# An attention block on one core: how the turned probabilities go through DRAM, and where values, transposes and the weighted sum stand

## The chip, the core and the metric

The kernel runs on one core of a Trainium2 chip. The metric is the device time of one execution in microseconds (us), as the median of several runs. A profile of one further execution shows when each engine worked: TensorE (PE, with its weight loads as PEld), VectorE (DVE), ScalarE (ACT), GpSimd (POOL) and SyncE (SP, which here issues DMAs only; its DMA queue is written SPq).

## What is computed

A transformer block on x of 32 sequences x 256 tokens x 256 features, with a context of 32 x 256 x 192: self attention, cross attention and a gated feed-forward part, 16 heads of 64, all in float32.

```python
h = _ln(x, g1, be1)
x = _attn(h, h, Wq1, Wk1, Wv1, Wo1, bo1) + x
h = _ln(x, g2, be2)
x = _attn(h, context, Wq2, Wk2, Wv2, Wo2, bo2) + x
h = _ln(x, g3, be3)
y = h @ Wp + bp
a, gate = (y[..., :FF_HID], y[..., FF_HID:])
x = a * jax.nn.gelu(gate, approximate=False) @ W2 + b2 + x
```

`_attn` projects q, k and v, takes the softmax of q k^T / 8 per head, weights v with it, and projects with Wo.

## The kernel before

Three parts run one after the other: `attention` for self attention (names begin with `self_`), `attention` again for cross attention (`cross_`), and `feed_forward` (`ff_`). The change touches `attention` alone. Most products are made of three matmuls on a high and a low part of each operand (`h_hi`, `h_lo` and so on), so each operand is copied once (the high part, on ScalarE) and subtracted once (the low part, on VectorE or GpSimd).

Each attention part goes over 32 sequences, and each sequence over 8 pairs of heads. One pair is one step, and all engines run the same list of steps (`sequences`): the first sequence (FIRST), a hardware loop over the middle ones (LOOP), the last (LAST), and a drain. In step p an engine works on several pairs at once, each at its own lag behind the projected pair: scores one step later, exponentials two, turn three (`TURNED`), load four (`LOADED`), weighted sum five (`WEIGHTED`), output projection six (`PROJECTED`). The order of the work on an engine is the order in which `step` writes it; engines meet by semaphores only.

The path of one pair, numbered s over the whole part:

- TensorE projects q and k into the one PSUM bank `ps_qk` (L640), 12 matmuls in self attention and 11 in cross. ScalarE copies it to `qk_hi` (L472), VectorE makes `qk_lo` (`low_parts`, L558). The next projection waits for `qk_lo`.
- TensorE makes the scores (L726), VectorE the negated maxima of each half (L549), ScalarE the exponentials and their sums (L412), VectorE the inverse of the sums (L574), GpSimd scales the probabilities, one half at a time (L379).
- VectorE transposes 32 x 32 blocks of both halves at once into `blocks`, which has two slots (`turn`, L568). The blocks have to change partitions, which goes through the DRAM tensor `turns`: SyncE stores the tile by four DMAs of 32 partitions each, in rows of 1 KB (`store_turn`, L301), and loads it back by one DMA of 128 partitions with rows of 4 KB into `probs_t`, a ring of four (`load_turn`, L309).
- TensorE makes the weighted sum (L744), ScalarE and VectorE its high and low part (L463, L585), TensorE the output projection (L704), which adds up over the 8 pairs in `ps_y`.

On SyncE a step is `load_turn` of pair s-1 and then `store_turn` of pair s. The load waits for the semaphore of the pair's stores, and everything on SyncE stands in one row, so the stores of pair s are not issued before the load of s-1 is.

V is projected in parts of a quarter of its columns and one of two tiles of tokens: `V_PARTS` lists for steps 0 to 6 what is made, one part each, both tiles in step 4, nothing in step 7. All use the bank `ps_misc`, from which ScalarE copies (`copy_v`, L451). The transposes of the next sequence's normalized input (step 6, L662) and context (step 5) use the same bank, after the V part of their step, so they wait for its copy.

For the next sequence, VectorE does `norm_stats` in step 2 and `norm_apply` in step 3, ScalarE `high_h` and `high_context` in step 7, GpSimd `low_h` and `low_context` in step 7, ahead of the two scalings, and the residual with its bias (`residual`, L360) right behind them.

Of the kernel before, what the change touches and what calls it, by code (L numbers as in the profile page):

```python
# [24 lines left out]
F32 = mybir.dt.float32  # L25
# [23 lines left out]
SCORES, EXPS, TURNED, LOADED, WEIGHTED, PROJECTED = 1, 2, 3, 4, 5, 6  # L49
# [7 lines left out]
V_PARTS = ((0, (0,)), (0, (1,)), (1, (0,)), (1, (1,)), (2, (0, 1)), (3, (0,)), (3, (1,)))  # L57
V_READY = (2, 4, 5, 7)
# [82 lines left out]
def attention(nc, tag, x_in, ctx_in, x_out, weights, bo, gamma, beta, prefetch, yout, y_stored, before):  # L141
# [7 lines left out]
    with ExitStack() as es:  # L149
# [50 lines left out]
        turns = nc.dram_tensor(tag + "turns", [RING, QUADS, QUAD, QUADS, TURN], F32).ap()  # L200
# [58 lines left out]
        def stored_count(b, q):  # L259

            return 16 * QUADS * (PAIRS // 2 * b + q // 2 + 1)
# [4 lines left out]
        def _(sp):  # L266
# [28 lines left out]
            def store_turn(b, p):  # L295

                s = PAIRS * b + p - TURNED
                slot = (p - TURNED) % RING
                sp.wait_ge(turned, s + 1)
                for i in range(QUADS):  # L300
                    sp.dma_start(turns[slot, :, :, i].rearrange("j k n -> k j n"),  # L301
                                 blocks[QUAD * i:QUAD * (i + 1), slot % 2].rearrange("k (j n) -> k j n", j=QUADS)
                                 ).then_inc(turn_stored[slot % 2], 16)

            def load_turn(b, p):
# [3 lines left out]
                sp.dma_start(probs_t[:, slot], turns[slot].rearrange("j k i n -> (j k) (i n)")  # L309
                             ).then_inc(turn_loaded[slot], 16)  # L310
# [22 lines left out]
        def _(pool):  # L333
# [28 lines left out]
            def step(b, p, part):  # L362
# [3 lines left out]
                if part in (FIRST, LOOP) and p == 7:  # L366
                    low_h(b + 1)
                    if cross:
                        low_context(b + 1)
                if part != DRAIN and p == PROJECTED + 1:  # L370
                    residual(b)
                if alive(part, p, EXPS):
# [3 lines left out]
                    for h in range(2):  # L376
                        pool.wait_ge(inv_ready, 2 * s + h + 1)
# [16 lines left out]
        def _(act):  # L394
# [50 lines left out]
            def copy_v(b, p):  # L445

                quarter, tiles = V_PARTS[p]
                act.wait_ge(v_done, len(V_PARTS) * b + p + 1)
# [6 lines left out]
            def step(b, p, part):  # L455
# [24 lines left out]
                if part != DRAIN and p < len(V_PARTS):  # L480
                    copy_v(b, p)
                if part in (FIRST, LOOP) and p == 6:
# [14 lines left out]
        def _(dve):  # L497
# [25 lines left out]
            def extras(b, p, part):  # L523
# [7 lines left out]
                if part in (FIRST, LOOP):  # L531
# [4 lines left out]
                    if p == 5 and cross:  # L536
# [40 lines left out]
            def step(b, p, part):  # L577
# [568 lines left out]
```

## Time and profile before

| what | us |
|---|---|
| median of 3 runs | 3448.78 |
| lowest and highest of them | 3444.27, 3453.83 |
| the profiled execution | 3446.99 |
| its span, first to last instruction | 3445.2 |
| self attention, first pair's store to last (issues) | 31.1 to 1392.1 |
| cross attention, first pair's store to last (issues) | 1433.9 to 2849.0 |

The span is what the rows further on divide up. "Busy" is the time in which an engine had an instruction running, matmuls overlapping one another. A wait names what ended it. An issue of a DMA on SPq takes SyncE some tenths of a microsecond; its landing is when its semaphore has its full count.

### The profile page before, as it was taken

The page shows a single profiled execution, that of the slowest core. Times are in us where ns is not written, and L with a number is a line of the kernel's source. Part 1 is how long each engine was busy: PE and PEld are TensorE (multiplying, and loading weights), DVE is VectorE, ACT ScalarE, POOL GpSimd, SP SyncE. Part 2 cuts the span into 40 slices and gives each one's busy share as a digit, 9 for nine tenths or more (in the row PEclk, how much of TensorE's full clock was granted, in tenths as well). Part 3 has the DMA queues.
Part 4 walks back from the last instruction along what each step waited for, and adds up shares of the span by engine and source line. Part 5 has one row for each costly group of instructions (what it writes and reads, how often), then busy time and mean ns, then how long its engine had stood idle before and what let it go on. Part 6 is the DMA issues. An engine that isn't in the chain of part 4 may idle for free. (4 is left out here: it accounts for less than half of the span.)

```text
span 3445.2 us, 81835 instructions
## 1 busy us (share of the span) xinstructions
PE 3157.5 (92%) x25600; PEld 2633.6 (76%) x25600; DVE 2473.8 (72%) x4811; ACT 1891.2 (55%) x6063; POOL 1362.1 (40%) x1295
## 2 busy tenths in 40 slices
PE   7999999999999999689889988899989887999999
PEld 6877888777888777577777777777777766888888
DVE  7777777777777777577777777777777775556555
ACT  6666666665666665456556566566656552233222
POOL 4444444444444444344444444444444441001010
PEclk9999999999999999799999999999999998999999
DMA  7676677767677766577677676777767762000010
GB/s 234 213 220 213 215 216 217 215 211 217 213 218 216 213 216 214 163 215 209 211 209 217 208 218 211 215 210 216 219 207 213 214 207 60 31 30 30 24 37 19
DMA packets 464425, 625.02 MB, mean 181 GB/s; under 512 B 57728, under 2 KB 397056, under 8 KB 464128
## 3 DMA queue, kind: packets, MB, share of 16 engines
q1 hardware_dynamic: 460256, 624.09, 59.4%
q10 hardware_dynamic: 4128, 0.41, 0.1%
q8 instruction: 23, 0.38, 0.0%
q14 instruction: 18, 0.15, 0.0%
HBM read 330.71 MB, written 293.60 MB: 181 GB/s over the span
## 5 line engine op out<-in xcount | busy, mean ns | idle before, releaser
L379 POOL TENSOR_TENSOR cross_probs<-cross_probs,cross_row_inv 128x512 f32<-128x512 f32 x512 | 531.7, 1048 | 586.1 <-DVE cross_row_inv L574 570.7
L379 POOL TENSOR_TENSOR self_probs<-self_probs,self_row_inv 128x512 f32<-128x512 f32 x512 | 531.9, 1049 | 542.2 <-DVE self_row_inv L574 542.0
L412 ACT ACTIVATE cross_probs<-cross_ps_s,cross_neg_max 128x256 f32<-128x256 f32 x1024 | 474.6, 473 | 69.2 <-DVE cross_neg_max L549 66.2
L412 ACT ACTIVATE self_probs<-self_ps_s,self_neg_max 128x256 f32<-128x256 f32 x1024 | 474.1, 472 | 43.8 <-DVE self_neg_max L549 41.0
L549 DVE TENSOR_REDUCE self_neg_max<-self_ps_s 128x2 f32<-128x512 f32 x512 | 327.7, 681 | 116.8 <-PE self_ps_s L726 116.3
L549 DVE TENSOR_REDUCE cross_neg_max<-cross_ps_s 128x2 f32<-128x512 f32 x512 | 327.8, 681 | 110.3 <-PE cross_ps_s L726 110.2
L568 DVE STREAM_TRANSPOSE self_blocks<-self_probs 128x1024 f32<-128x1024 f32 x256 | 316.5, 1236 | 111.3 <-POOL self_probs L379 108.7
L568 DVE STREAM_TRANSPOSE cross_blocks<-cross_probs 128x1024 f32<-128x1024 f32 x256 | 316.5, 1237 | 103.1 <-POOL cross_probs L379 100.5
L744 PE MATMUL cross_ps_o<-cross_probs_t,cross_v 128*64 128x256 f32 x2048 | 283.6, 398 | 72.2 <-DMA cross_probs_t<-cross_turns 71.8
L463 ACT ACTIVATE cross_o_hi<-cross_ps_o 128x256 fp32r<-128x256 f32 x256 | 98.5, 385 | 447.8 <-PE cross_ps_o L744 447.8
L463 ACT ACTIVATE self_o_hi<-self_ps_o 128x256 fp32r<-128x256 f32 x256 | 98.5, 385 | 391.7 <-PE self_ps_o L744 391.7
L744 PE MATMUL self_ps_o<-self_probs_t,self_v 128*64 128x256 f32 x2048 | 281.0, 395 | 18.2 <-DMA self_probs_t<-self_turns 17.8
L950 ACT ACTIVATE ff_u_hi<-ff_gated 128x512 fp32r<-128x512 f32 x128 | 81.0, 632 | 300.9 <-PE ff_ps_y L1090 214.2
L744 PEld LDWEIGHTS cross_ps_o<-cross_probs_t,cross_v 128*64 128x64 f32 x2048 | 132.2, 138 | 146.4 <-issue 64.2
L640 PE MATMUL cross_ps_qk<-cross_h_hi,cross_hi_wq 128*128 128x256 f32 x512 | 172.0, 336 | 44.1 <-DVE cross_qk_lo L558 39.0
L910 POOL TENSOR_TENSOR ff_xres<-ff_xt,ff_b 128x1024 f32<-128x1024 f32 x16 | 38.5, 2406 | 437.5 <-DMA out<-ff_yout 437.5
L412 ACT ACTIVATION_READ_ACCUMULATOR cross_probs<-cross_ps_s,cross_neg_max 128x1 f32 x1024 | 210.4, 206 | 0.0
L640 PE MATMUL self_ps_qk<-self_h_hi,self_hi_wq 128*128 128x256 f32 x512 | 172.5, 337 | 41.1 <-DVE self_qk_lo L558 33.0
L412 ACT ACTIVATION_READ_ACCUMULATOR self_probs<-self_ps_s,self_neg_max 128x1 f32 x1024 | 209.8, 205 | 0.0
L640 PEld LDWEIGHTS cross_ps_qk<-cross_h_hi,cross_hi_wq 128*128 128x128 f32 x512 | 97.3, 190 | 146.6 <-issue 97.9
L1034 DVE TENSOR_TENSOR ff_u_lo<-ff_gated,ff_u_hi 128x512 fp32r<-128x512 f32 x128 | 115.8, 904 | 129.4 <-ACT ff_u_hi L950 129.4
L640 PEld LDWEIGHTS self_ps_qk<-self_h_hi,self_hi_wq 128*128 128x128 f32 x512 | 97.4, 190 | 142.7 <-issue 99.7
(166 smaller groups left out, 10332.6 us busy)
## 6 DMA issues: line engine op xcount, KB each, us to landing
self_turns<-self_blocks SPq DMA_DIRECT2D x1024, 128.0 KB, 3.5
self_probs_t<-self_turns SPq DMA_DIRECT2D x256, 512.0 KB, 3.8
cross_turns<-cross_blocks SPq DMA_DIRECT2D x1024, 128.0 KB, 3.5
cross_probs_t<-cross_turns SPq DMA_DIRECT2D x256, 512.0 KB, 3.8
self_xt<-in_x SPq DMA_DIRECT2D x32, 256.0 KB, 3.4
self_xres<-in_x SPq DMA_DIRECT2D x32, 256.0 KB, 3.8
after_self_attention<-yout SPq DMA_DIRECT2D x32, 256.0 KB, 3.6
cross_xt<-after_self_attention SPq DMA_DIRECT2D x32, 256.0 KB, 3.9
```

The source lines that it names most:

```text
L379: pool.tensor_tensor(probs[:, slot % 2, h], probs[:, slot % 2, h], scale, ALU.mult).then_inc(probs_ready, 1)
L412: last = act.activation(probs[:, slot % 2, h, t], scores[:, slot % 2, h, t], ACT.Exp, bias=neg_max[:, slot % 2, i:i + 1], accum_out=row_su ...
L463: act.activation(o_hi[:, slot], ps_o[:, 0:SEQ], ACT.Copy).then_inc(o_hi_ready, 1)
L549: nc.vector.tensor_reduce(neg_max[:, slot, r], scores[:, slot, h], AX_X, ALU.max, negate=True).then_inc(neg_max_ready, 1)
L568: nc.vector.transpose(blocks[:, slot % 2].rearrange("p (j a q) -> p a j q", j=QUADS, q=QUAD), probs[:, slot % 2].rearrange("p h t (k j q) ...
L640: last = nc.tensor.matmul(out, m[:, p * P:(p + 1) * P], a, start=i == 0, stop=i == len(passes) - 1)
L744: last = nc.tensor.matmul(ps_o[DHEAD * h:DHEAD * (h + 1), 0:SEQ], v[:, k, c:c + DHEAD], turned_t[:, h, k], start=k == 0, stop=k == TT - 1)
L910: pool.tensor_tensor(xres[:], xt[:, parity], bias, ALU.add).then_inc(xres_ready, 1)
L950: act.activation(u_hi[:, slot], gated[:, slot], ACT.Copy).then_inc(u_hi_ready, 1)
L1034: nc.vector.tensor_tensor(u_lo[:, slot], gated[:, slot], u_hi[:, slot].bitcast(F32), ALU.subtract).then_inc(u_ready, 1)
```

## The change

- `turns` gets the layout of the tile itself. The store is one DMA of 128 partitions in rows of 4 KB. The load is four DMAs of 32 partitions each, in rows of 1 KB, and does the change of partitions.
- `WEIGHTED` is 6 and `PROJECTED` 7, so the weighted sum and all behind it come one pair later, and the drain has seven steps. The result (`yout`) and what goes with it on SyncE move along.
- V is made in six parts at steps 0, 1, 2, 4, 6 and 7: steps 2 and 4 make both tiles, steps 3 and 5 none. The transposes of the context are in step 3 and those of h in step 5; the V part behind each waits until `ps_misc` has been read.
- Within the projections of h, the terms with `h_lo` are last, and TensorE waits for `h_lo` only ahead of them, in the first step of a sequence.
- On VectorE `turn` stands behind `low_parts`.
- On GpSimd `low_h` and `low_context` stand between the two scalings of step 7, and `residual` stands in step 2 of the next sequence.

```diff
-SCORES, EXPS, TURNED, LOADED, WEIGHTED, PROJECTED = 1, 2, 3, 4, 5, 6
+SCORES, EXPS, TURNED, LOADED, WEIGHTED, PROJECTED = 1, 2, 3, 4, 6, 7
...
-V_PARTS = ((0, (0,)), (0, (1,)), (1, (0,)), (1, (1,)), (2, (0, 1)), (3, (0,)), (3, (1,)))
-V_READY = (2, 4, 5, 7)
+V_PARTS = ((0, (0,)), (0, (1,)), (1, (0, 1)), (2, (0, 1)), (3, (0,)), (3, (1,)))
+V_STEPS = (0, 1, 2, 4, 6, 7)
+V_READY = (2, 3, 4, 6)
+TURN_CONTEXT, TURN_H = 3, 5
...
-        turns = nc.dram_tensor(tag + "turns", [RING, QUADS, QUAD, QUADS, TURN], F32).ap()
+        turns = nc.dram_tensor(tag + "turns", [RING, P, QUADS * TURN], F32).ap()
...
-                for i in range(QUADS):
-                    sp.dma_start(turns[slot, :, :, i].rearrange("j k n -> k j n"),
-                                 blocks[QUAD * i:QUAD * (i + 1), slot % 2].rearrange("k (j n) -> k j n", j=QUADS)
-                                 ).then_inc(turn_stored[slot % 2], 16)
+                sp.dma_start(turns[slot], blocks[:, slot % 2]).then_inc(turn_stored[slot % 2], 16)
...
-                sp.dma_start(probs_t[:, slot], turns[slot].rearrange("j k i n -> (j k) (i n)")
-                             ).then_inc(turn_loaded[slot], 16)
+                for j in range(QUADS):
+                    sp.dma_start(probs_t[QUAD * j:QUAD * (j + 1), slot].rearrange("k (i n) -> k i n", i=QUADS),
+                                 turns[slot].rearrange("(i k) (j n) -> j k i n", k=QUAD, j=QUADS)[j]
+                                 ).then_inc(turn_loaded[slot], 16)
...
-                if part in (FIRST, LOOP) and p == 7:
-                    low_h(b + 1)
-                    if cross:
-                        low_context(b + 1)
-                if part != DRAIN and p == PROJECTED + 1:
-                    residual(b)
+                if part != FIRST and p == 2:
+                    residual(b - 1)
...
+                        if part in (FIRST, LOOP) and p == 7 and h == 1:
+                            low_h(b + 1)
+                            if cross:
+                                low_context(b + 1)
...
-                if alive(part, p, TURNED):
-                    turn(b, p)
                 if alive(part, p, EXPS):
                     inverse(g - EXPS, (p - EXPS) % RING, 0)
                 if part != DRAIN:
                     low_parts(g, p)
+                if alive(part, p, TURNED):
+                    turn(b, p)
...
-                        yield h_lo[:, k], hi[:, k]
-                        yield h_hi[:, k], lo[:, k]
...
+                if part in (FIRST, LOOP) and p == TURN_H + 1:
+                    pe.wait_ge(h_t_ready, b + 2)
...
-                    pe.wait_ge(h_ready, b + 1)
+                    pe.wait_ge(h_hi_ready, b + 1)
```

Three places of the order in which the instructions stand. The first is SyncE's queue in self attention, around the loads and stores of two pairs of the first sequence. Before:

```order
L301 DMA self_turns<-self_blocks 32x4x256 x4
L309 DMA self_probs_t<-self_turns 128x1024
L301 DMA self_turns<-self_blocks 32x4x256 x4
L309 DMA self_probs_t<-self_turns 128x1024
L301 DMA self_turns<-self_blocks 32x4x256 x4
```

Now:

```order
L302 DMA self_turns<-self_blocks 128x1024
L309 DMA self_probs_t<-self_turns 32x4x256 x4
L302 DMA self_turns<-self_blocks 128x1024
L309 DMA self_probs_t<-self_turns 32x4x256 x4
L302 DMA self_turns<-self_blocks 128x1024
```

The four issues of a pair have moved from the store to the load; the turn of store and load is as it was.

The second is VectorE in self attention, one step of the first sequence that has all of a plain step's work. Before:

```order
L585 TENSOR_TENSOR self_o_lo<-self_ps_o,self_o_hi 128x256
L568 STREAM_TRANSPOSE self_blocks<-self_probs 128x8x4x32
L574 RECIPROCAL self_row_inv<-self_row_sum 128x2
L558 TENSOR_TENSOR self_qk_lo<-self_ps_qk,self_qk_hi 128x512
L574 RECIPROCAL self_row_inv<-self_row_sum 128x2
L549 TENSOR_REDUCE self_neg_max<-self_ps_s 128x2 x2
```

Now:

```order
L587 TENSOR_TENSOR self_o_lo<-self_ps_o,self_o_hi 128x256
L576 RECIPROCAL self_row_inv<-self_row_sum 128x2
L560 TENSOR_TENSOR self_qk_lo<-self_ps_qk,self_qk_hi 128x512
L570 STREAM_TRANSPOSE self_blocks<-self_probs 128x8x4x32
L576 RECIPROCAL self_row_inv<-self_row_sum 128x2
L551 TENSOR_REDUCE self_neg_max<-self_ps_s 128x2 x2
```

The transpose has moved behind the first inverse and the low parts, and ahead of the second inverse.

The third is GpSimd in self attention, the end of the loop over sequences (steps 6 and 7; register rows belong to the waits). Before:

```order
L379 TENSOR_TENSOR self_probs<-self_probs,self_row_inv 128x512
L346 TENSOR_TENSOR self_h_lo<-self_h_t,self_h_hi 128x512
L357 REGISTER_ALU
L358 REGISTER_ALU
L360 TENSOR_TENSOR self_xres<-self_xres,self_bo 128x512
L377 ISA
L379 TENSOR_TENSOR self_probs<-self_probs,self_row_inv 128x512
L377 REGISTER_ALU
L379 TENSOR_TENSOR self_probs<-self_probs,self_row_inv 128x512
```

Now:

```order
L380 TENSOR_TENSOR self_probs<-self_probs,self_row_inv 128x512
L378 ISA
L380 TENSOR_TENSOR self_probs<-self_probs,self_row_inv 128x512
L347 TENSOR_TENSOR self_h_lo<-self_h_t,self_h_hi 128x512
L378 REGISTER_ALU
L380 TENSOR_TENSOR self_probs<-self_probs,self_row_inv 128x512
```

`h_lo` now stands between the two scalings of step 7, and the residual has left this place for step 2.

## Rows read from the trace of the kernel before

**Rows 1.** The page's busy us (share of the span) and instructions of each engine.
```profile
PE 3157.5 (92%) x25600; PEld 2633.6 (76%) x25600; DVE 2473.8 (72%) x4811; ACT 1891.2 (55%) x6063; POOL 1362.1 (40%) x1295
```
**Rows 2.** SyncE queue's waits: engine line, waited for, us in total, times, longest us.
```profile
SPq L309 <- DMA cross_turns<-cross_blocks: 685.1, 255, 4.5
SPq L309 <- DMA self_turns<-self_blocks: 672.4, 256, 4.1
...
SPq L301 <- DVE cross_blocks L568: 24.9, 13, 18.5
SPq L301 <- DVE self_blocks L568: 20.4, 16, 14.4
```
**Rows 3.** Lines 309 and 301: issue ns, first and last start; landings of 301.
```profile
L309 SPq DMA_DIRECT2D self_probs_t<-self_turns x256: 333/338/347, 34.8 to 1395.4; - x128
L309 SPq DMA_DIRECT2D cross_probs_t<-cross_turns x256: 337/338/350, 1439.0 to 2852.3; - x128
...
DMA to landing us min/median/max: 2.0/3.5/5.2
```
**Rows 4.** SyncE's timeline in self attention: start, us, engine, line, what, count.
```profile
701.12 0.34 SPq L309 DMA_DIRECT2D self_probs_t<-self_turns  x1
701.57 1.80 SPq L301 DMA_DIRECT2D self_turns<-self_blocks  x4
706.58 0.34 SPq L309 DMA_DIRECT2D self_probs_t<-self_turns  x1
...
711.76 0.34 SPq L309 DMA_DIRECT2D self_probs_t<-self_turns  x1
```
**Rows 5.** DMA issues: size of one, median us from issue to landing.
```profile
self_probs_t<-self_turns SPq DMA_DIRECT2D x256, 512.0 KB, 3.8
...
out<-ff_yout SPq DMA_DIRECT2D x16, 512.0 KB, 3.0
```
**Rows 6.** Windows of 1 us: PE, PEld, DVE, ACT, POOL; PEclk, DMA share, GB/s.
```profile
704.00:705.00 1.00, 1.00 (x11) 1.00 (x9) 0.81 (x3) 1.00 (x4) 0.66 (x1) 1.00 1.00 362
...
706.00:707.00 1.00, 1.00 (x10) 0.48 (x8) 0.92 (x6) 0.00 (x0) 0.78 (x2) 1.00 0.02 6
```
**Rows 7.** Timelines of GpSimd, VectorE, TensorE at a sequence's first step, in brackets idle before.
```profile
689.18 1.28 POOL L346 TENSOR_TENSOR self_h_lo<-self_h_t,self_h_hi 128x512 fp32r<-128x512 f32 x1 [4.42 <-ACT self_h_hi L434]
...
693.06 2.04 POOL L379 TENSOR_TENSOR self_probs<-self_probs,self_row_inv 128x512 f32<-128x512 f32 x2
...
695.25 1.25 DVE L568 STREAM_TRANSPOSE self_blocks<-self_probs 128x1024 f32<-128x1024 f32 x1 [3.51 <-POOL self_probs L379]
...
697.18 0.39 PE L640 MATMUL self_ps_qk<-self_h_hi,self_hi_wq 128*128 128x256 f32 x1 [1.58 <-DVE self_qk_lo L558]
```
**Rows 8.** TensorE's timeline: transposes of one sequence, starts of steps in self and cross.
```profile
683.77 0.66 PE L662 MATMUL self_ps_misc<-self_ident,self_xnorm 128*128 128x128 f32 x4 [0.47 <-ACT self_v L451]
...
702.11 0.39 PE L640 MATMUL self_ps_qk<-self_h_hi,self_hi_wq 128*128 128x256 f32 x1
...
707.05 0.38 PE L640 MATMUL self_ps_qk<-self_h_hi,self_hi_wq 128*128 128x256 f32 x1
...
2129.51 0.39 PE L640 MATMUL cross_ps_qk<-cross_h_hi,cross_hi_wq 128*128 128x256 f32 x1 [1.14 <-DVE cross_qk_lo L558]
...
2134.22 0.38 PE L640 MATMUL cross_ps_qk<-cross_h_hi,cross_hi_wq 128*128 128x256 f32 x1
```
**Rows 9.** Timelines of VectorE and ScalarE within a plain step of self attention.
```profile
702.99 1.24 DVE L568 STREAM_TRANSPOSE self_blocks<-self_probs 128x1024 f32<-128x1024 f32 x1
...
703.83 0.60 ACT L472 ACTIVATE self_qk_hi<-self_ps_qk 128x512 fp32r<-128x512 f32 x1 [0.31 <-PE self_ps_qk L640]
704.32 0.47 ACT L412 ACTIVATE self_probs<-self_ps_s,self_neg_max 128x256 f32<-128x256 f32 x1
704.46 0.69 DVE L558 TENSOR_TENSOR self_qk_lo<-self_ps_qk,self_qk_hi 128x512 fp32r<-128x512 f32 x1 [0.19 <-ACT self_qk_hi L472]
...
706.63 1.28 DVE L549 TENSOR_REDUCE self_neg_max<-self_ps_s 128x2 f32<-128x512 f32 x2
```

More of the change, by code:

```diff
@@ L259, in stored_count @@
         def stored_count(b, q):
-            return 16 * QUADS * (PAIRS // 2 * b + q // 2 + 1)
+            return 16 * (PAIRS // 2 * b + q // 2 + 1)
         block = es.enter_context(nc.Block())
@@ L445, in copy_v @@
             def copy_v(b, p):
-                quarter, tiles = V_PARTS[p]
-                act.wait_ge(v_done, len(V_PARTS) * b + p + 1)
+                i = V_STEPS.index(p)
+                quarter, tiles = V_PARTS[i]
+                act.wait_ge(v_done, len(V_PARTS) * b + i + 1)
                 if counts(c := PAIRS * (b - 1) + 2 * quarter + 2):
@@ L479, in step @@
                     exps(g - EXPS, (p - EXPS) % RING, 1)
-                if part != DRAIN and p < len(V_PARTS):
+                if part != DRAIN and p in V_STEPS:
                     copy_v(b, p)
-                if part in (FIRST, LOOP) and p == 6:
+                if part in (FIRST, LOOP) and p == TURN_H:
                     scale_shift(b + 1)
@@ L535, in extras @@
                         norm_apply(b + 1)
-                    if p == 5 and cross:
+                    if p == TURN_CONTEXT and cross:
                         context_copy(b + 1)
@@ L626, in terms @@
                         yield h_hi[:, k], hi[:, k]
+                        yield h_hi[:, k], lo[:, k]
+                    for k in range(KT):
                         yield h_lo[:, k], hi[:, k]
-                        yield h_hi[:, k], lo[:, k]
                 else:
@@ L635, in terms, with project_pair @@
                     yield c_hi[:, 1], lo[:, 1]
-            def project_pair(out, p, source_h, w):
+            def project_pair(out, p, source_h, w, h_count=None):
                 passes = list(terms(source_h, w))
                 for i, (a, m) in enumerate(passes):
+                    if h_count is not None and i == 2 * KT:
+                        pe.wait_ge(h_ready, h_count)
                     last = nc.tensor.matmul(out, m[:, p * P:(p + 1) * P], a, start=i == 0, stop=i == len(passes) - 1)
@@ L643, in project_v @@
             def project_v(b, p, part):
-                quarter, tiles = V_PARTS[p]
-                if counts(c := len(V_PARTS) * b + p):
+                i = V_STEPS.index(p)
+                quarter, tiles = V_PARTS[i]
+                if counts(c := len(V_PARTS) * b + i):
                     pe.wait_ge(v_ready, c)
-                if cross and part in (FIRST, LOOP) and p == 6:
+                if cross and part in (FIRST, LOOP) and p == TURN_CONTEXT + 1:
                     pe.wait_ge(c_t_ready, b + 2)
+                if part in (FIRST, LOOP) and p == TURN_H + 1:
+                    pe.wait_ge(h_t_ready, b + 2)
                 if part == FIRST and p == 0:
@@ L651, in project_v @@
                 passes = list(terms(not cross, "wv"))
-                for i, t in enumerate(tiles):
+                for n_t, t in enumerate(tiles):
                     for j, (a, m) in enumerate(passes):
-                        last = nc.tensor.matmul(ps_misc[:, i * V_COLS:(i + 1) * V_COLS], a[:, t * P:(t + 1) * P],
+                        last = nc.tensor.matmul(ps_misc[:, n_t * V_COLS:(n_t + 1) * V_COLS], a[:, t * P:(t + 1) * P],
                                                 m[:, quarter * V_COLS:(quarter + 1) * V_COLS],
@@ L667, in transpose_h @@
                 pe.wait_ge(xnorm_ready, b + 1)
-                if counts(c := len(V_PARTS) * b):
+                if counts(c := len(V_PARTS) * b - 2):
                     pe.wait_ge(v_ready, c)
@@ L689, in step @@
                     project_pair(ps_qk[:, SEQ:2 * SEQ], p, not cross, "wk").then_inc(qk_done, 1)
-                if part != DRAIN and p < len(V_PARTS):
+                if part != DRAIN and p in V_STEPS:
                     project_v(b, p, part)
@@ L709, in step @@
                 if part in (FIRST, LOOP):
-                    if p == 5 and cross:
+                    if p == TURN_CONTEXT and cross:
                         transpose_context(b + 1)
-                    if p == 6:
+                    if p == TURN_H:
                         transpose_h(b + 1)
```

6 lines of the change are left out of this document (3 added, 3 removed).

## Prediction

> **What bounds the kernel now.** I read the busy table first. TensorE is busy 92% of the span [rows 1], which looks like the bound, but matmuls overlap in that figure, so it only says that TensorE is rarely idle for long. I then asked the DMA queue of SyncE (SP) what it waits for. The queue waits for the landing of a turned pair's stores before 255 of 256 loads in each attention part, 672.4 and 685.1 us in all. It waits for the vector engine to produce a turned pair only 16 and 13 times, 20.4 and 24.9 us, most of it once per part while the pipeline fills [rows 2]. So the queue is a chain of its own that hardly ever runs dry: load pair s-1, store pair s, wait until the store has landed, load pair s, and so on. Its mean cycle follows from the first and last of 256 loads: (1395.4 - 34.8)/255 = 5.336 us in self attention and (2852.3 - 1439.0)/255 = 5.542 us in cross attention [rows 3]. Two times 255 of these are 2774 us, four fifths of the span.
>
> What one cycle is made of stands in the queue's timeline [rows 4]. The load is issued at 701.12, the four stores start at 701.57 and take 1.80 to issue (so the last starts 1.37 later, at a spacing of 0.457), and the next load starts at 706.58. A plain cycle is the next one, 706.58 to 711.76, 5.18 us. The mean is longer by 0.16 (self) and 0.36 (cross), because the transfers of the sequence (input, residual, context, result) run in the same queue. Of the plain 5.18, 0.45 + 1.37 = 1.82 is issue, and 3.36 is the wait for the last quarter store, whose median landing is 3.5 and whose shortest is 2.0 [rows 3].
>
> TensorE is close behind. A step (one pair) that waits for nothing takes 707.05 - 702.11 = 4.94 us in self and 2134.22 - 2129.51 = 4.71 in cross, each with one part of V in it; there are eight such parts to eight pairs. The transposes add 0.66 per sequence in self, twice that in cross [rows 8]. So its floor is 4.94 + 0.66/8 = 5.02 and 4.71 + 1.32/8 = 4.88 us per pair, below the queue's 5.336 and 5.542 by 0.31 and 0.67.
>
> **Seams, V parts, order of engines.** At the first step of each sequence TensorE stands 1.58 us until qk_lo [rows 7]. The chain behind that: GpSimd does h_lo (from 689.18) and the residual before the two scalings (693.06, 2.04 us), VectorE's turn waits for them 3.51 us and runs 695.25 to 696.50, and low_parts stands behind the turn. The change puts low_parts ahead of turn, the first scaling ahead of h_lo and the residual elsewhere, so this stall should go. It moves the context and h transposes to steps that have no V part, where they need not wait for a copy, and lets the first four Q matmuls run before h_lo. All of this shortens TensorE's path, by roughly 1 to 2 us per sequence. On the queue's path it is worth only the moments in which the queue ran dry: 20.4 + 24.9 less the fill (14.4 and 18.5, the longest of each) = 12.4 us [rows 2]. That is the whole gain that I allow for these edits, since the queue covers the rest; if the queue became faster, up to the floors above would be free.
>
> What they cost: turn now starts behind low_parts, some 2 us later in its step (702.99 against the end of low_parts at 705.15 [rows 9]), and inverse of the second half, yout and the maxima stand behind it. The readers of these are GpSimd's second scaling and ScalarE's next exponentials. The store waits for turn, but the queue reaches it later anyway. In the fill of each part nothing hides those 2 us, and the last quarter load starts 1.37 after the first: at most 3.6 us per part, 7 in all. Net of these small terms: -12 + 7 = -5 us.
>
> **Weighted sum one pair later.** It adds no instruction within the loop, gives a load 4.9 us more before TensorE reads it, and lengthens the drain by a step that does a few matmuls. As long as the queue's cycle is above TensorE's, slack only lets the backlog grow until turn waits for its free block; it doesn't raise the rate. Cost and gain: nothing, beyond what is counted.
>
> **Stores and loads.** The same bytes and five issues per pair remain, but four of them now belong to the load. The new cycle is: first load issue to store issue, 3 x 0.457 + 0.47 = 1.84 us (the form with 4 x 32 rows of 1 KB is today's store form), and then L, the landing of one store of 512 KB. So the cycle is 1.84 + L against 5.18, and break-even is L = 3.34. The trace has no such store behind four small loads, so I bound L. Below: a 512 KB store with nothing ahead lands in 3.0 us [rows 5], cycle 4.84. Above: from 128 KB in 2.0 [rows 3] and 512 KB in 3.0, the data of 512 KB take 1.33 and the fixed part is 1.67; a 512 KB load takes 3.8 [rows 5], 0.8 more than a store. Today 3.8 + 1.33 = 5.13 explains the 5.18: the stores queue behind the load. In the same way the last quarter load lands at 1.37 + 2.0 + 0.8 = 4.17 at worst, and the store 1.33 later: 5.50. Between the ends (-0.34 and +0.32) I take 3.0 + 0.2 = 3.2, cycle 5.04, gain 0.14 us. The reason is the occupancy of the DMA engines: they are full from 704 to 705 but at 0.02 of their time from 706 to 707, before the next load [rows 6], so more than a microsecond of each cycle is latency and not bytes. The new store is issued when three of the quarters have had time to run, and has about one (0.33 us of data, in part done) before it; today's last store has the whole load and three stores.
>
> The Trainium skill, "DMA: Bandwidth & Descriptors", section "Anatomy of one DMA — SWDGE (gpsimd) path", gives about 2.0 us plus bytes over 436 GB/s for the GpSimd path, which estimates 3.2 us for 512 KB where the trace has 3.0 for SyncE's queue; with the 0.2 above the cycle would be 5.24 and the sum some 31 us worse than today's instead of better. The row decides for me.
>
> **Sum.** 2 x 255 x 0.14 = 71.4 us, plus 5 of the small terms: 76 us off the profiled execution. That execution took 3447.0 us (span 3445.2 and 1.8 around it), 1.8 under the median of the three runs. 3447.0 - 76 = 3371. The feed-forward part is untouched.
>
> **Rivals.**
> Cycle unchanged: L comes out at 3.34, because the engine that serves a load last also ends its share of the store last, so that the bytes of one cycle set its length in either cut. The estimate of 5.13 above, which fits today's cycle, is of this kind. All seam edits are then hidden: 3447 - 5 = 3442. Against it: the idle microsecond [rows 6].
> Slower: the load in quarters holds the queue longer than the stores in quarters did, since loads land 0.8 later than stores of their size [rows 5], and each quarter starts its reads anew. The point from which it decides is L above 3.34; at L = 3.5, today's median for a quarter store with much ahead of it [rows 3], the cycle is 5.34: 510 x 0.16 = 82, so 3447 + 82 - 5 = 3524. The same page of the Trainium skill, section "Rules for kernel authors", speaks against this half of the change: transfers to disjoint parts of the partitions serialize, and one transfer over 128 partitions is to be used. Today's stores spaced 0.457 apart [rows 4] do not contradict it.
> Another engine takes over: L is near 3.0 or less, and the compute engines set the pace. In the new order VectorE and ScalarE form a ring: exponentials of a half (2 x 0.47), qk_hi 0.60, qk_lo 0.69, turn 1.24, inverse and hand-overs about 0.3, first maximum 0.64: 4.4 us per pair [rows 9], plus normalization and context copy in some steps. With that about 5.05 and 5.0 per pair in the two parts: 255 x (0.29 + 0.54) = 212, so 3235 at best; with L at 3.0 the queue still sets 5.2 in cross and TensorE 5.02 in self, 255 x (0.316 + 0.34) = 167, so 3275.
>
> **How the numbers follow.** This kernel's runs differ by some 0.3%, which is what a measurement can tell from no change. Chances: my forecast (cycle shorter by 0.03 to 0.3) 0.60; cycle unchanged 0.13; slower 0.19; another engine as bound 0.08. Faster: 0.60 + 0.08 = 0.68, same 0.13, slower 0.19. The range goes from 3290 (a gain just short of L = 3.0) to 3510 (cycle 0.13 longer); I leave out 0.08 below and about 0.12 above.
>
> **What would show it.** In the profile after, first and last load starts give the cycle: 5.20 and 5.40 us if I am right, about 5.34 and 5.54 if nothing was won. SP should still wait for the landing before nearly every load; the landing of the 512 KB store should be 3.2 to 3.4 in the median, the stall before qk at the first step should be gone, and TensorE's waits for probs_t too. I am wrong if SP waits for VectorE's turn in most cycles (then the queue is no longer the bound), or if the landing is above 3.7.

## The result

The changed kernel takes 3500.82 us in the median (3498.13 to 3503.24) against 3451.31 of the kernel before (3444.27 to 3456.17): a ratio of 1.0145, with a 95% interval of 1.0124 to 1.0165. It is slower by 1.5%; the forecast was 3371, faster by 2.2%. The profiled execution has a span of 3501.4 us against 3445.2, 56.2 us more.

The page of the changed kernel, busy table and DMA slices, which answer to [rows 1]:

```profile
PE 3229.6 (92%) x25600; PEld 2669.6 (76%) x25600; DVE 2463.3 (70%) x4811; ACT 1879.0 (54%) x5999; POOL 1366.8 (39%) x1295
...
DMA  6666666666666666566666666666666662101010
```

TensorE's share is the same 92%, and the DMA engines are less busy, with the same bytes. Neither says what happened. The waits of SyncE's queue do (after, columns as in [rows 2]):

```profile
SPq L309 <- DMA self_turns<-self_blocks: 746.4, 256, 5.1
SPq L309 <- DMA cross_turns<-cross_blocks: 710.5, 255, 4.4
...
SPq L302 <- DVE cross_blocks L570: 24.0, 9, 20.8
SPq L302 <- DVE self_blocks L570: 17.3, 6, 15.5
```

The queue now waits for a landing before all but one of the loads of its 512 pairs. Beyond the fill of each part it waits for VectorE some 5 us in all (17.3 + 24.0 less 15.5 and 20.8; 12.4 before). So it is the pace even more purely than before. The stores of the changed kernel (line 302, as in [rows 3]; below the starts stands who waited for the stores, in us and times, and then their landing):

```profile
L302 SPq DMA_DIRECT2D self_turns<-self_blocks x256: 332/358/437, 31.8 to 1439.0; - x128
L302 SPq DMA_DIRECT2D cross_turns<-cross_blocks x256: 344/359/437, 1484.7 to 2902.8; - x128
...
  DVE self_blocks L570: 188.7, 178
  DVE cross_blocks L570: 166.6, 182
...
DMA to landing us min/median/max: 2.6/3.6/5.6
```

That VectorE waits for the stores is new: turn finds both of its blocks still unstored. TensorE's waits have moved, too (after; engine, line, what it waited for, us in total, times, longest): those of the first steps for qk_lo, 1.58 us once per sequence before [rows 7], are gone, and the output projection waits for o_lo, which stands behind the held turn on VectorE.

```profile
PE self_ps_y L712 <- DVE self_o_lo L587: 87.0, 59, 2.8
...
PE self_ps_qk L645 <- DVE self_qk_lo L560: 4.1, 4, 1.4
```

The cycle is (1439.0 - 31.8)/255 = 5.518 us in self attention (5.336 before) and (2902.8 - 1484.7)/255 = 5.561 in cross (5.542). Where the 56.2 us came from follows from the same starts and those of the stores before (31.1, 1392.1, 1433.9, 2849.0): self attention's 255 cycles 1407.2 - 1361.0 = 46.2, the passage from the last store of self to the first of cross 45.7 - 41.8 = 3.9, cross attention 1418.1 - 1415.1 = 3.0, the end 598.6 - 596.2 = 2.4, the start 0.7. One cycle in the timeline of the changed kernel, which answers to [rows 4]:

```profile
741.60 1.73 SPq L309 DMA_DIRECT2D self_probs_t<-self_turns  x4
743.52 0.34 SPq L302 DMA_DIRECT2D self_turns<-self_blocks  x1
747.02 1.73 SPq L309 DMA_DIRECT2D self_probs_t<-self_turns  x4
748.86 0.36 SPq L302 DMA_DIRECT2D self_turns<-self_blocks  x1
752.41 1.73 SPq L309 DMA_DIRECT2D self_probs_t<-self_turns  x4
```

From load to store 748.86 - 747.02 = 1.84 us, as forecast; from store to the next load 752.41 - 748.86 = 3.55 us, forecast 3.2. The plain cycle is 5.39 us instead of 5.18. These are single cycles. Over all cycles without another transfer in them (between 100 and 1350 us, and between 1500 and 2800), the median of the starts on SyncE's timeline is 5.24 us before and 5.42 now in self attention, and 5.28 and 5.44 in cross: the plain cycle has grown by some 0.17 us in both parts.

### The profile page after: what moved, and what is told of

It reads as the page before. It is cut to its first block and busy times, and to the rows that moved or that the text cites. A ratio compares the mean times of both kernels' runs of the same rounds, so it can differ in the third digit from the quotient of the medians.

```text
span 3501.4 us, 81867 instructions
## 1 busy us (share of the span) xinstructions
PE 3229.6 (92%) x25600; PEld 2669.6 (76%) x25600; DVE 2463.3 (70%) x4811; ACT 1879.0 (54%) x5999; POOL 1366.8 (39%) x1295
## 3 DMA queue, kind: packets, MB, share of 16 engines
q1 hardware_dynamic: 460256, 624.09, 56.2%
## 5 line engine op out<-in xcount | busy, mean ns | idle before, releaser
L752 PE MATMUL cross_ps_o<-cross_probs_t,cross_v 128*64 128x256 f32 x2048 | 295.5, 412 | 6.6 <-DMA cross_probs_t<-cross_turns 6.6
L752 PE MATMUL self_ps_o<-self_probs_t,self_v 128*64 128x256 f32 x2048 | 293.2, 409 | 5.8 <-DMA self_probs_t<-self_turns 5.2
L560 DVE TENSOR_TENSOR self_qk_lo<-self_ps_qk,self_qk_hi 128x512 fp32r<-128x512 f32 x256 | 177.0, 692 | 122.7 <-ACT self_qk_hi L474 122.7
L712 PE MATMUL cross_ps_y<-cross_hi_wo,cross_o_hi 128*128 128x256 f32 x512 | 161.3, 315 | 103.0 <-DVE cross_o_lo L587 102.3
L560 DVE TENSOR_TENSOR cross_qk_lo<-cross_ps_qk,cross_qk_hi 128x512 fp32r<-128x512 f32 x256 | 177.0, 691 | 112.1 <-ACT cross_qk_hi L474 108.6
L712 PE MATMUL self_ps_y<-self_hi_wo,self_o_hi 128*128 128x256 f32 x512 | 155.9, 304 | 88.1 <-DVE self_o_lo L587 87.0
```

What stands on the lines that cost most here:

```text
L560: nc.vector.tensor_tensor(qk_lo[:, slot], ps_qk[:], qk_hi[:, slot].bitcast(F32), ALU.subtract).then_inc(qk_ready, 1)
L712: last = nc.tensor.matmul(ps_y[:, t * DIM:(t + 1) * DIM], a[:, q % 2, t * P:(t + 1) * P], m[:, q], start=q == 0 and t == 0 and i == 0, sto ...
L752: last = nc.tensor.matmul(ps_o[DHEAD * h:DHEAD * (h + 1), 0:SEQ], v[:, k, c:c + DHEAD], turned_t[:, h, k], start=k == 0, stop=k == TT - 1)
```

## The experiments

Theory Q is the prediction's: SyncE's queue is the pace, and the time goes with its cycle. The rivals are named where they are tested. The first four experiments ran on a chip on which the kernel before takes 3482.37 us; on those of the others it takes 3452. Ratios are to the kernel before on the same chip.

### 1 and 2: the form of the DMAs alone

Experiment 1 is the changed kernel with stores and load of before.

```diff
-                sp.dma_start(turns[slot], blocks[:, slot % 2]).then_inc(turn_stored[slot % 2], 16)
+                for i in range(QUADS):
+                    sp.dma_start(turns[slot, :, :, i].rearrange("j k n -> k j n"),
...
-                for j in range(QUADS):
+                sp.dma_start(probs_t[:, slot], turns[slot].rearrange("j k i n -> (j k) (i n)")
```

> The changed kernel with one part undone: four quarter stores and one whole load per pair, as before the change; V parts, transposes, order of engines and the later weighted sum stay changed. Theory Q (SyncE's queue sets the pace, and the change lost because the cycle with four loads and one store is 5.38 us in a plain step against 5.18): the cycle goes back to about 5.3 and 5.5 us and the time to 3440 us (3420 to 3460), some 60 below the changed kernel. Rival E (the new order of the engines is what costs: turn behind low_parts, and normalization in step 3 ahead of the maxima, make a ring of VectorE and ScalarE the pace, and the queue only follows): 3485 to 3505, as the changed kernel.

Measured: 3467.76 us, ratio 0.9958 (0.9945 to 0.9971). Experiment 2 is the opposite, the kernel before with the new stores and loads only.

> The kernel before with one part of the change alone: one whole store and four quarter loads per pair. Theory Q: slower, 3500 us (3480 to 3530), SyncE's cycle 5.4 to 5.6 us, and TensorE waits for probs_t more often than before, since the weighted sum is not moved. Rival E: 3440 to 3460, as before.

Measured: 3508.79 us, ratio 1.0077 (1.0053 to 1.0102). The two are compared with the kernel before on one chip. The new DMAs alone cost it 0.8%, 26 us; all the rest of the change, under the old form, is a gain of 0.4%, 15 us. Both signs speak for Q and against rival E: the loss lies in the form of the DMAs. TensorE waits for `probs_t` 264 times in experiment 2, against 107 before, as expected. Experiment 1 took 3467.76 us where I had said 3420 to 3460, which on this slower chip is no miss of the gain; but its cycle was not met in self attention: (1429.3 - 32.7)/255 = 5.477 us where I had said 5.3, and (2875.4 - 1474.4)/255 = 5.494 in cross (experiment 1):

```profile
L303 SPq DMA_DIRECT2D self_turns<-self_blocks x1024: 302/433/2269, 32.7 to 1429.3; - x171
L303 SPq DMA_DIRECT2D cross_turns<-cross_blocks x1024: 303/433/1500, 1474.4 to 2875.4; - x171
```

How much the form costs together with the rest is not settled, since the changed kernel did not run on this chip. Its ratio of 1.0145 against experiment 1's 0.9958 makes it 1.9%, some 65 us; its time of 3500.82 us against 3467.76 makes it 33 us. The two differ by the 30 us that the kernel before takes longer on this chip, and experiment 2's 26 us stand nearer to the second. The cycles of experiment 2, (1442.8 - 30.8)/255 = 5.537 and (2906.6 - 1487.4)/255 = 5.566 us, are those of the changed kernel:

```profile
L300 SPq DMA_DIRECT2D self_turns<-self_blocks x256: 336/357/437, 30.8 to 1442.8; - x128
L300 SPq DMA_DIRECT2D cross_turns<-cross_blocks x256: 344/359/439, 1487.4 to 2906.6; - x128
```

### 3 and 4: the store ahead of the load

```diff
-                if alive(part, p, LOADED):
-                    load_turn(b, p)
                 if alive(part, p, TURNED):
                     store_turn(b, p)
+                if alive(part, p, LOADED):
+                    load_turn(b, p)
```

> The changed kernel with two calls exchanged on SyncE: in each step the store of pair s is issued before the queue waits for and issues the load of pair s-1, so that no store waits for a landing any more. Nothing else differs, not even the DMAs themselves. Theory Q: the queue stops setting the pace, SyncE's wait for landings shrinks to little and the wait for turn takes its place; TensorE's floor of about 5.0 us per pair comes in sight: 3260 us (3220 to 3330). Rival E: no gain, 3480 to 3505, since the engines' ring stays as it is.

Measured: 3197.05 us, ratio 0.9183 (0.9160 to 0.9206), 8% faster than the kernel before and below the 3220 to 3330 that I expected. Against the changed kernel nothing but two calls on SyncE changed places. The queue's waits in experiment 3:

```profile
SPq L302 <- DVE self_blocks L570: 515.2, 252, 15.3
...
SPq L302 <- DVE cross_blocks L570: 445.4, 221, 20.6
...
SPq L309 <- DMA cross_turns<-cross_blocks: 4.7, 5, 1.7
...
SPq L309 <- DMA self_turns<-self_blocks: 3.7, 3, 1.6
```

And its line 302:

```profile
L302 SPq DMA_DIRECT2D self_turns<-self_blocks x256: 319/338/727, 32.9 to 1302.7; - x128
L302 SPq DMA_DIRECT2D cross_turns<-cross_blocks x256: 337/338/466, 1348.7 to 2594.0; - x128
DMA to landing us min/median/max: 2.6/3.0/5.3
```

The wait for landings has gone from some 700 us in each part to 4.7 and 3.7, and a wait for turn has taken its place. The cycle is (1302.7 - 32.9)/255 = 4.98 us in self and (2594.0 - 1348.7)/255 = 4.88 in cross: near the floors of TensorE that the prediction worked out, 5.02 and 4.88 (the first was a little too high). In a window of 900 us of cross attention TensorE is busy for 898.94 of them (experiment 3; columns as in [rows 6]):

```profile
1600.00:2500.00 900.00, 898.94 (x7911) 741.42 (x7911) 754.56 (x1542) 614.11 (x2071) 473.62 (x461) 1.00 0.83 241
```

> The kernel before with the same two calls exchanged on SyncE. Theory Q: faster, but the stalls at the first step of a sequence (about 1.5 us of TensorE behind turn) and before the transposes (0.6 each) now stand on the path, and a load has less time before its weighted sum: 3370 us (3300 to 3430). If the queue's chain was not what bounded the kernel before, 3440 to 3460.

Measured: 3535.50 us, ratio 1.0142 (1.0112 to 1.0172): slower, against my expectation. The queue waits for turn here too, but the timeline shows another loop (experiment 4, self attention):

```profile
706.64 0.36 SPq L309 DMA_DIRECT2D self_probs_t<-self_turns  x1
...
706.79 1.08 PE L744 MATMUL self_ps_o<-self_probs_t,self_v 128*64 128x256 f32 x8
707.92 0.38 ACT L463 ACTIVATE self_o_hi<-self_ps_o 128x256 fp32r<-128x256 f32 x1 [1.96 <-PE self_ps_o L744]
708.34 0.42 DVE L585 TENSOR_TENSOR self_o_lo<-self_ps_o,self_o_hi 128x256 fp32r<-128x256 f32 x1
708.68 1.24 DVE L568 STREAM_TRANSPOSE self_blocks<-self_probs 128x1024 f32<-128x1024 f32 x1
709.94 1.76 SPq L301 DMA_DIRECT2D self_turns<-self_blocks  x4
711.73 0.63 PEld L744 LDWEIGHTS self_ps_o<-self_probs_t,self_v 128*64 128x64 f32 x8
...
711.74 0.44 SPq L309 DMA_DIRECT2D self_probs_t<-self_turns  x1
```

A weighted sum (706.79) is followed by its high and low part, by the turn that stands behind them on VectorE, by that pair's stores, and only then by the load (711.74) for the weighted sum two steps on, which lands 4.5 us later in the median. That is 4.95 us from the sum to the load and, from the load at 706.64 to its own sum at 711.73, 5.09: 10.04 for two steps, 5.02 each where nothing else delays them. Over the whole part the loads start every (1454.4 - 38.0)/255 = 5.55 us (from their first and last starts); which steps add the rest I did not itemize, but TensorE's waits for this load are the largest it has. Issuing the store first makes the load later, and at lag 5 there is no room for that.

### 5 to 7: what counts when the queue is not the pace

> The changed kernel with the store ahead of the load in each step on SyncE (as the third experiment), and in addition the DMAs of before: four quarter stores and one whole load per pair. Theory Q: where the queue does not set the pace, the form of the DMAs is worth nothing: the same time as the third experiment within 0.3% (ratio to the kernel before 0.918). Rival D (the form of the DMAs costs by itself, by load on the memory or the DMA engines): 1 to 2% apart, as the forms were 60 us apart in the first experiment.

Measured: 3203.56 us, ratio 0.9282 (0.9265 to 0.9299). By the ratio this is 1.1% above experiment 3, as rival D has it; by the time it is within 0.2% of it. The two ran on different chips, and on this one the kernel before is 30 us faster. For the time as the right measure speaks that the traces agree where no landing holds up TensorE: the stretch from the last store of cross attention to the end is 3194.7 - 2594.0 = 600.7 us in experiment 3 and 3202.6 - 2602.4 = 600.2 in this one, and the cycles are (1302.7 - 32.2)/255 = 4.98 and (2602.4 - 1352.6)/255 = 4.90 us against 4.98 and 4.88. So the form of the DMAs is worth little or nothing here, and what it costs in experiments 1 and 2 comes through the queue's cycle. These two kernels were not run on one chip.

Experiment 6 puts the weighted sum back.

```diff
-SCORES, EXPS, TURNED, LOADED, WEIGHTED, PROJECTED = 1, 2, 3, 4, 6, 7
+SCORES, EXPS, TURNED, LOADED, WEIGHTED, PROJECTED = 1, 2, 3, 4, 5, 6
```

> The third experiment (store first) with the weighted sum and the projection moved back to lags 5 and 6. Theory W: with the store first a load is issued behind the next pair's turn, and a weighted sum at lag 5 closes a loop of two steps: weighted sum, high and low part, turn, store, load, weighted sum, about 11 us or more with the turn late in its step, so 5.5 to 6 us per pair: 3500 to 3650 us on a chip where the kernel before takes 3450 to 3480. If the later weighted sum does not matter, 3200.

Measured: 3525.74 us, ratio 1.0213 (1.0194 to 1.0231). TensorE's waits for the load are back (experiment 6):

```profile
PE cross_ps_o L752 <- DMA cross_probs_t<-cross_turns: 165.9, 214, 3.8
...
PE self_ps_o L752 <- DMA self_probs_t<-self_turns: 134.8, 180, 3.9
```

So the later weighted sum is worth over 300 us once the store is issued first. Neither of the two brings this alone: the store first without it is slower than the kernel before (experiments 4 and 6). With the load first, it is a part of experiment 1, where the whole rest of the change gains 15 us; by itself it was not tried.

Experiment 7 is experiment 3 with the old order on VectorE and GpSimd.

```diff
+                if alive(part, p, TURNED):
+                    turn(b, p)
                 if alive(part, p, EXPS):
                     inverse(g - EXPS, (p - EXPS) % RING, 0)
                 if part != DRAIN:
                     low_parts(g, p)
-                if alive(part, p, TURNED):
-                    turn(b, p)
```

> The third experiment with the order of the engines of before: on VectorE turn ahead of the first inverse and the low parts, on GpSimd low_h and low_context ahead of both scalings. V in six parts, the moved transposes, the later weighted sum and the residual's place stay. Where the queue is not the pace these seams stand on the path: the stall of TensorE at a sequence's first step (1.6 us in self, 1.1 in cross) comes back, 62 sequences: +60 to +110 us, 3260 to 3310. If the new order is what makes the ring of VectorE and ScalarE slow, the time falls below 3190 instead.

Measured: 3164.23 us, ratio 0.9168 (0.9151 to 0.9185). This is 33 us below experiment 3, which differs in the order alone but ran on another chip, and 39 us below experiment 5, which ran on the same chip but has the old DMAs. My 60 to 110 us of loss were wrong, and so was my belief in the new order: with the queue out of the way it costs. The same window in experiment 7, and then its line 302:

```profile
1600.00:2500.00 900.00, 900.00 (x8041) 749.35 (x8039) 790.65 (x1570) 622.40 (x2100) 478.68 (x467) 1.00 0.84 245
```

```profile
L302 SPq DMA_DIRECT2D self_turns<-self_blocks x256: 320/338/344, 30.0 to 1293.9; - x128
L302 SPq DMA_DIRECT2D cross_turns<-cross_blocks x256: 337/338/487, 1337.7 to 2561.7; - x128
```

TensorE does 8041 matmuls in the 900 us in which it did 7911 in experiment 3, 1.6% more, though "busy" says almost 100% in both: overlapping matmuls hide small gaps. The cycles are 4.96 and 4.80 us, and these 510 cycles are 27 of the 32 us between the spans of experiments 3 and 7 (3194.7 and 3162.4, on two chips). This is the fastest kernel of the study, 8.3% below the one before. Which of the two orders costs, VectorE's or GpSimd's, was not parted.

### 8 and 9: why the store lands late

Experiment 8 lays `turns` out as quarter, partition, column, so that the store has rows of 1 KB and a quarter lies in one piece.

```diff
-                sp.dma_start(turns[slot], blocks[:, slot % 2]).then_inc(turn_stored[slot % 2], 16)
+                sp.dma_start(turns[slot].rearrange("j p n -> p j n"),
+                             blocks[:, slot % 2].rearrange("p (j n) -> p j n", j=QUADS)
...
-                                 turns[slot].rearrange("(i k) (j n) -> j k i n", k=QUAD, j=QUADS)[j]
+                                 turns[slot, j].rearrange("(i k) n -> k i n", k=QUAD)
```

> The changed kernel, load first as it was, with the tile stored by one DMA in rows of 1 KB instead of 4 KB (turns in DRAM as quarter, partition, column; the quarter loads read rows of 1 KB that lie behind one another). Theory Q1: the store lands 3.6 us after its issue because it queues behind the quarter loads (without them in front it took 3.0 in the third experiment), and the size of the rows matters little: landing 3.5 to 3.8 us, time within 1% of the changed kernel. Rival Q2: rows of 4 KB written to DRAM are what lands late: landing 3.3 or less, time 40 us or more below the changed kernel.

Measured: 3431.98 us, ratio 0.9942 (0.9925 to 0.9960), 2% below the changed kernel. The DMA groups of experiment 8, and its line 302:

```profile
self_turns<-self_blocks SPq DMA_DIRECT2D x256, 512.0 KB, 3.4
self_probs_t<-self_turns SPq DMA_DIRECT2D x1024, 128.0 KB, 2.7
```

```profile
L302 SPq DMA_DIRECT2D self_turns<-self_blocks x256: 376/377/2108, 31.9 to 1399.8; - x128
```

Both landings are shorter by 0.2 us, and the cycle is (1399.8 - 31.9)/255 = 5.364 us. My expectation that the rows matter little was wrong, but two things had changed, the stored rows and the place of the rows that a quarter load reads. Experiment 9 keeps the layout of the change and leaves 64 bytes free behind each KB, which forces rows of 1 KB on the store.

```diff
-        turns = nc.dram_tensor(tag + "turns", [RING, P, QUADS * TURN], F32).ap()
+        turns = nc.dram_tensor(tag + "turns", [RING, P, QUADS, TURN + 16], F32).ap()
```

> The changed kernel with 64 bytes left free behind every 1 KB of the DRAM tensor, so that the store goes out in rows of 1 KB as in the eighth experiment, while a quarter load still reads rows that lie about 4 KB apart, as in the changed kernel. It parts what the eighth changed together. Theory R (reading each quarter from rows 4 KB apart is what holds the queue: quarter loads land in 2.9 us against 2.7 when their rows lie together, and the store behind them starts that much later): quarter loads again 2.9 us, SyncE's cycle 5.5 us, time within 0.5% of the changed kernel (ratio to before 1.01 to 1.02). Theory S (the size of the stored rows is what counts): loads 2.7, cycle 5.36 to 5.44, ratio 0.994.

Measured: 3565.24 us, ratio 1.0326 (1.0302 to 1.0350), slower than either theory said. Experiment 9's DMA groups and its line 302:

```profile
self_turns<-self_blocks SPq DMA_DIRECT2D x256, 512.0 KB, 3.7
self_probs_t<-self_turns SPq DMA_DIRECT2D x1024, 128.0 KB, 2.8
```

```profile
L302 SPq DMA_DIRECT2D self_turns<-self_blocks x256: 518/520/1548, 31.5 to 1468.7; - x128
```

The gap brought a cost of its own: the issue of the store takes 520 ns, where the same rows without the gap took 377 (experiment 8), and the cycle is 5.636 us. Neither theory has its numbers. That the rows of 1 KB by themselves did not bring the time of experiment 8 speaks against theory S and for the place of a quarter's rows in DRAM. But the gap also puts the rows at multiples of 1088 bytes instead of 1024, and its cost may have hidden what the rows are worth; so why experiment 8 is faster is not shown.

### 10: the order of the engines under the queue

> The changed kernel, load first, with the order of before on VectorE (turn ahead of the first inverse and low parts) and GpSimd (low_h and low_context ahead of both scalings): the seventh experiment without the exchange on SyncE. Theory Q: while SyncE's queue is the pace the engines' order is covered, the 34 to 40 us that it was worth in the seventh are not seen: ratio to before 1.010 to 1.018, as the changed kernel, cycle 5.5 us. If the order counts here too: 1.002 to 1.006.

Measured: 3497.00 us, ratio 1.0124 (1.0102 to 1.0147), overlapping the changed kernel's 1.0145. The 33 to 39 us that the order is worth in experiment 7 are covered by the queue.

### 11: the landing with one quarter load ahead

```diff
-                for j in range(QUADS):
+                for j in range(1):
```

> The changed kernel with only the first of the four quarter loads issued; the other three quarters of the turned probabilities are left out (they stay zero), so the output is not the reference's. It shows the landing L of the whole-tile store with one quarter load ahead of it instead of four. Theory Q: L falls from 3.6 to about 3.0 to 3.1 us, the cycle to 0.47 + 3.1 = 3.6 us if nothing else bounds it, so the queue waits for turn and the time is TensorE's, 3200 us. If L stays at 3.5 or more, the loads ahead are not what delays it.

Measured: one execution, 3189.85 us. The kernel leaves out three of the four quarter loads, so only its landings count here. The store's group, and one pair of its timeline (experiment 11):

```profile
self_turns<-self_blocks SPq DMA_DIRECT2D x256, 512.0 KB, 2.6
```

```profile
741.82 0.32 SPq L309 DMA_DIRECT2D self_probs_t<-self_turns  x1
744.13 0.33 SPq L302 DMA_DIRECT2D self_turns<-self_blocks  x1
746.77 0.32 SPq L309 DMA_DIRECT2D self_probs_t<-self_turns  x1
```

The landing is 2.6 us, below my 3.0 to 3.1. But more than the number of loads has changed. The queue waits for turn here, so the store is issued 2.3 us after the one quarter load ahead of it (2.0 in the median), which itself lands in 2.5, and from 744 to 745 the DMA engines are busy for 0.07 of their time. So 2.6 us is the landing with next to nothing ahead. In experiment 3 the last of four quarter loads is issued some 2.7 us before the next store and takes 3.6 to land, so it is still on its way: 3.0. In the changed kernel it is issued 0.47 before: 3.6. The runs show a later landing with more work in front of it; how much of it each single load brings, they do not part.

## Why the prediction was wrong

**The bound: right.** The queue's cycle sets the time of the changed kernel. Experiment 3 shows it: the same DMAs and the same instructions on every engine, the store no longer held by a landing, and 8.7% less time. For the kernel before it rests on the queue's waits [rows 2] and on experiment 2, in which the DMAs alone move cycle and time; experiment 4 does not test it, since another loop takes over there at once. Two readings of the prediction were a little off: self attention has 256 waits of 256 and not 255, and the plain cycle of 5.18 us is a single one, where the median is 5.24.

**The step that failed: L.** The prediction put it as "Between the ends (-0.34 and +0.32) I take 3.0 + 0.2 = 3.2, cycle 5.04, gain 0.14 us". Measured is 3.6 in the median and a plain cycle of 5.39. Both terms of the 3.2 were off, in opposite ways. The base was 3.0, from a store in rows of 1 KB [rows 5]; the whole tile in rows of 4 KB lands in 2.6 with next to nothing ahead (experiment 11). The queueing was 0.2; behind four quarter loads it is 3.6 - 2.6 = 1.0. I argued from the empty microsecond before each load [rows 6] that most of a cycle is latency and that the store would find the DMA engines nearly free. The empty microsecond is still there (changed kernel):

```profile
750.00:751.00 1.00, 1.00 (x10) 1.00 (x10) 0.67 (x3) 1.00 (x5) 0.09 (x1) 1.00 1.04 333
...
752.00:753.00 1.00, 1.00 (x16) 0.79 (x16) 0.58 (x1) 1.00 (x5) 1.00 (x1) 1.00 0.00 0
```

It stands between one landing and the first bytes of the next load, and says nothing about the time between the first load and the store's landing, in which the DMA engines of the changed kernel are at 0.87, 1.04 and 0.66 of their time from 749 to 752. The other estimate of the prediction, by queueing, ran from 5.13 to 5.50 us and held the 5.39. The two ends were there, and I chose by the wrong row. The landing by which I would have called myself wrong, above 3.7, was also set too high: by my own break-even of 3.34, the 3.6 is enough. And that 3501 lies within 3290 to 3510 is owed to the width of that range and not to its reasons.

**The rival that won: slower.** It had its mechanism (the load in quarters holds the queue longer), its point (L above 3.34), and at L = 3.5 it gave 3524; the kernel took 3501 with L a little above that, since in cross attention the mean cycle rose by 0.02 us only. The plain cycle rose there by 0.16 as well; what shrank is the price of the sequence's own transfers, which I had carried over unchanged. It stands in one cycle of each sequence above all, the one behind the loads of the next input and context. Its mean over 29 sequences is 6.68 us in the kernel before and 5.77 now, which is (6.68 - 5.77)/8 = 0.11 us per pair. One such cycle, 2133.93 to 2140.62 (before):

```profile
2133.93 0.35 SPq L309 DMA_DIRECT2D cross_probs_t<-cross_turns  x1
2134.39 2.09 SPq L301 DMA_DIRECT2D cross_turns<-cross_blocks  x4
2140.62 0.34 SPq L309 DMA_DIRECT2D cross_probs_t<-cross_turns  x1
```

Why the new form has less of this was not tried.

**Two rules on the form of DMAs.** The Trainium skill, "DMA: Bandwidth & Descriptors", section "Rules for kernel authors", has one transfer over 128 partitions rather than two over disjoint halves, because the halves serialize. Each form here has one transfer cut by partitions, the old one the store and the new one the load, so experiments 1 and 2 do not decide on this rule; they only show that the new form costs more than the old. The Trainium skill, same page, section "Anatomy of one DMA — SWDGE (gpsimd) path", has a fit of about 2.0 us plus bytes over 436 GB/s for the path of GpSimd; an estimate by it is 3.2 us for this store. The traces have 2.6 to 3.6 on SyncE's queue, by what stands in front of it.

**Seams, V parts, order: covered, as said,** but for the wrong reason in one point. The stall of 1.58 us at a sequence's first step [rows 7] did not come back when the old order was restored under the store-first queue (experiment 7). So the new order is not needed to remove it. What does was not parted: in self attention the store-first queue alone takes most of it away (TensorE's waits for `qk_lo` are 7.4 us in experiment 4 and 33.0 before), in cross attention it does not (25.7 and 39.0). The new order costs time: 33 to 39 us in experiment 7, nothing where the queue covers it (experiment 10). The ring of VectorE and ScalarE that the prediction named is where it may come from; that is argued, not shown.

**Weighted sum one pair later: nothing, as said,** as far as the runs show: it has no run of its own, and the rest of the change that holds it gains 15 us (experiment 1). In VectorE's new waits for the stores one sees the slack turned into backlog, up to the two blocks. What I did not see is that this slack is the condition for issuing the store first, and that the gain lay there (experiments 3 and 6).

## What to carry to other kernels

Look for a queue whose every wait is for its own transfers: its cycle, from first and last start divided by the count, is the pace of the kernel, however busy the compute engines look. Before changing the form of such transfers, ask whether the wait has to stand in the cycle at all; here two calls in another order took the changed kernel from 3501 to 3197 us, where recutting the same transfers had made it slower. Then ask whether what moves later still has room: with the weighted sum one pair earlier, the same two calls cost 1.4%. When a transfer is moved behind others in one queue, price it with their bytes ahead of it, and take a landing from a row that has the same work in front at the same distance.

## What the runs showed of the hardware

- One store of 512 KB in rows of 4 KB lands in 2.6 us (median) with the DMA engines nearly idle (experiment 11), in 3.0 with the last of four 128 KB loads issued some 2.7 us ahead (experiment 3), and in 3.6 with it issued 0.47 us ahead (changed kernel). A store of 512 KB in rows of 1 KB took 3.0 in the feed-forward part [rows 5].
- The issue of a 512 KB store takes SyncE 358 ns in rows of 4 KB (changed kernel), 377 in rows of 1 KB (experiment 8) and 520 in rows of 1 KB with 64 bytes left free behind each in DRAM (experiment 9).
- The kernel before took 3452 us on two chips and 3482 on another. What differs between them was not found. Not every kernel differs by as much: experiment 2 took 3509 us on the one with 3482, and the changed kernel, whose cycles are the same within 0.02 us, 3501 where the kernel before takes 3451.
- The mean granted clock was 0.980 before, 0.962 after and 0.981 in experiment 10, which takes the changed kernel's time. So the lower clock of the changed kernel is not what it lost by.
